# Rotary attention stage: exponentials of one PSUM bank each in six units, with products and pieces placed by counting banks

## The chip, the cores and the metric

One core of one Trainium2 chip. The metric is the device time of one execution in microseconds (us). Three runs of the kernel before gave 1812.57, 1814.32 and 1814.37 us, median 1814.32.

## The reference

Four layers run one after the other on x of 4 batches x 1024 tokens x 128 channels: a causal linear attention, a switch attention (expert gates on queries, keys and values), a rotary attention, and a feed-forward layer applied to the half of the tokens that a router picks. Each is added to x (the last one replaces the chosen tokens) and layer-normalised. The change lies in the third:

```python
q, k, v = (x @ W + b).reshape(B, S, 16, 8).transpose(0, 2, 1, 3)   # for Wq, Wk, Wv
q, k = apply_rope(q, rope), apply_rope(k, rope)
scores = einsum('bhqd,bhkd->bhqk', q, k) / sqrt(8)
attn = softmax(scores, axis=-1)
out = einsum('bhqk,bhkd->bhqd', attn, v)          # then @ Wo + bo
```

So 4 batches x 16 heads have a 1024 x 1024 matrix of scores each, every element of which is exponentiated.

## The kernel before

All four layers run in one program, and the rotary stage begins while the stage ahead of it ends. Its inner loop computes transposed scores: a **tile** is 128 keys by 512 queries of one head, which is one bank of PSUM (the accumulator memory: 8 banks of 128 partitions x 512 fp32). A **step** is one block of 128 keys (`kt`) against one half of the queries for a group of four heads, so four tiles. There are 8 steps for a half, 16 for a group, 64 for a batch and 256 in all: 1024 tiles.

- **TensorE scores** (`score_unit`, L2660): one matmul for a tile, of 32 rows (8 channels in four split copies) by 128 columns. The four heads of a step use the four row groups of the array, so matmuls issued together run beside each other. A *unit* is two tiles in two neighbouring banks; `unit_b` has three of them in banks 0 to 5, and the score of unit u waits for the exponential of unit u-3 (`exp_rdy`).
- **ScalarE exponentials** (L2604): one instruction of 128x1024 for a unit, out of the two banks into `probs`, a ring of four steps (16 tiles). The first unit of each step (c = 0) stands behind two waits, on `pv_done` (the ring is free) and on `score_ps` (the scores are there); the second (c = 1) has only the one on `score_ps`.
- **TensorE products** (`products`, L2674): for a step four matmuls 128 x 32 columns into the four quarters of bank 6 (`acc_b`), accumulated over the 8 key blocks of a half. They are fp32, and the trace shows each as two. The products of two steps are issued together at every even step, for the two steps before it.
- **The slot between**: at every odd step TensorE has one more item in bank 7 (`piece_b`): a `turn` (L2686, four transposes of the accumulated result, at step 3 of every 8) or a `piece`, one of the small matmul groups that prepare the next batch (its transposes, q, k, v projections), finish the batch before (project_out) or rank its tokens. The first batch also carries pieces of the stage before, two of which hold 24 matmuls (L2283). Pieces wait on `used`, which VectorE raises when it has taken the last content of bank 7.
- **VectorE** copies bank 6 to `acc` after every 8 steps (L2799), normalises, takes the pieces and does the layer norm of the batch before. **GpSimd** lays out `vg`. **SyncE** writes the rotated q and k to DRAM (L2382) and reads them back by group (L2387, `staged`), where reading waits for a count of `score_ps`.

TensorE's order in `batch`, for a step i: score unit (i, c=1), score unit (i+1, c=0); if i is even the products of steps i-2 and i-1; if i is odd the turn or piece. TensorE runs its queue in order, and so does ScalarE. Two steps (four units, eight tiles) make one **cycle** of this order, counted below from the start of one block of products to the next: products, two score units, the item of the slot, two score units.

Before the first score of the second unit, `tail.banks_left` waits until the stage before has left the banks.

Of the kernel before, what the change touches and what calls it, by code (L numbers as in the profile page):

```python
# [16 lines left out]
ACT = mybir.ActivationFunctionType  # L17
# [2284 lines left out]
class RotaryLead:  # L2302
# [5 lines left out]
              + [("v", 0), ("v", 1)])  # L2308
    AT = {(0, 1): (0, 1), (0, 2): (2, 3), (0, 3): (4, 5), (1, 0): (6, 7), (1, 1): (8, 9), (1, 2): (10, 11)}
    ROPE_STEPS = 2 * 2 * 5  # L2310
    COUNTS = B * 8 * NT

    def __init__(self, nc, signals, x, ps, ident, I, tag):
        self.nc, self.x, self.I, self.ident, self.bank = nc, x, I, ident, ps[:, 0, :]
        self.base = self.end = nc.sbuf_base
        self.tag = tag
        sem, sb = signals.names(tag), self.place
        self.wq, self.wk, self.wv, self.wo, self.wq_sw, self.wk_sw = (sb(n, [P, D]) for n in ("wq", "wk", "wv", "wo", "wq_sw", "wk_sw"))
        self.b_col = sb("b_col", [P, 4])
        self.b_all = sb("b_all", [P, 2, D])  # L2320
        self.spared = self.end - self.base
        self.cos, self.sin = sb("cos", [P, T]), sb("sin", [P, T])
        self.xT = sb("xT", [P, T])
        self.rot, self.part = sb("rot", [P, HALF]), sb("part", [P, HALF])
        self.split = sb("split", [P, 4, T], F32R)
        self.keys = sb("keys", [P, 2, T], F32R)
        self.queries = sb("queries", [P, 2, T], F32R)
        self.vg = [sb("vg0", [P, NT, self.G, 32])]
        self.v = sb("v", [P, B * NT, D])
        self.needs = self.end - 4 * (B - 1) * NT * D  # L2330
        self.vg.append(sb("vg1", [P, NT, self.G, 32]))
        self.probs = sb("probs", [P, 4, 2, 2, HALF])
        self.acc, self.ao = sb("acc", [P, 2, HALF]), sb("ao", [P, NT, D])
        self.needs_later = self.end
        self.heads = nc.dram_tensor(tag + "heads", [B, 2, H, 4, HD, T], F32).ap()
# [113 lines left out]
def rotary_led(nc, x, ps, ident, place, signals, lead, tail, weights_of, recips, flag, I, tag):  # L2449
# [25 lines left out]
    with ctx:  # L2475
# [26 lines left out]
        SC = 2 * STEPS  # L2502
        NORM_STEPS = LN_STEPS + 1
        ROPE_STEPS = lead.ROPE_STEPS
        DMAS = 2
# [14 lines left out]
        def pieces(b, first, last):  # L2520
# [9 lines left out]
                at.update({PIECE_STEPS[NZ + NX + k]: (d_index(b, k), kind, half, b - 1) for k, (kind, half) in enumerate(D_PIECES)})  # L2530
            return at

        def turned_at(b, i):

            return b * NP + (i - TURN) // NT if i >= TURN else max(b * NP - 1, 0)
# [71 lines left out]
        def _(pe):  # L2607
            pe.sem_inc(score_ps, ONE + SC)
            pe.sem_inc(pv_done, ONE + STEPS)
            def piece(index, kind, half, b, turned=0):  # L2610

# [34 lines left out]
            def score_unit(step, c):  # L2646

                b, i = step // BS, step % BS
                g, half, kt = i // STEPS, i // NT % 2, i % NT
                par, u = g % 2, 2 * step + c  # L2650
                if i % STEPS == 0 and c == 0:
                    pe.wait_ge(staged[par], 16 * DMAS * (b * (NG // 2) + g // 2 + 1))

                if u == 1:
# [3 lines left out]
                for s in range(2):  # L2658
                    at = 32 * (2 * c + s)
                    last = nc.tensor.matmul(unit_b[u % NU][:, s, :], keys[at:at + 32, par, kt * P:(kt + 1) * P], queries[at:at + 32, par, half * HALF:(half + 1) * HALF], start=True, stop=True)  # L2660
                last.then_inc(score_ps, 1)

            def products(b, i):

                par, kt, pair = i // STEPS % 2, i % NT, i // NT
                pe.wait_ge(exp_rdy, ONE + 2 * (b * BS + i) + 2)
                if i % STEPS == 0:
                    pe.wait_ge(vg_rdy, ONE + G * (b * NG + i // STEPS + 1))
                if kt == 0:

                    pe.wait_ge(acc_sb, ONE + b * NP + pair)
                for hh in range(G):
                    at = 32 * hh
                    last = nc.tensor.matmul(acc_b[at:at + 32, :], vg[par][:, kt, hh, :], probs[:, kt % 4, hh // 2, hh % 2, :],  # L2674
                                            start=(kt == 0), stop=(kt == NT - 1))
                last.then_inc(pv_done, 1)

# [10 lines left out]

            pe.wait_ge(used, NX)

            def batch(b, first, last):
                at = pieces(b, first, last)
                for i in range(BS):
                    step = b * BS + i
                    score_unit(step, 1)
                    if step + 1 < B * BS:
                        score_unit(step + 1, 0)
                    if i % 2 == 0 and step:
                        for back in (2, 1):
                            products(*((b, i - back) if i else (b - 1, BS - back)))  # L2700
                    if i % NT == TURN and not (first and i == TURN):
                        turn(*((b, i // NT - 1) if i > TURN else (b - 1, NP - 1)), (NX if first else z_index(b, 0)) + sum(j < i for j in at))
                    if i in at:
                        piece(*at[i], turned_at(b, i))

            score_unit(0, 0)
            batches(pe, batch)
            for back in (2, 1):
                products(B - 1, BS - back)

            def left():
                turn(B - 1, NP - 1, z_index(B, 0) - NX)
# [736 lines left out]
```

## Time and profile before

| | before |
|---|---|
| median of 3 runs | 1814.32 us |
| the profiled execution's own time | 1811.27 us |
| its span, first to last instruction | 1809.5 us |
| granted TensorE clock, mean | 0.978 |
| TensorE busy | 1661.8 us (92%) |
| ScalarE busy | 1272.4 us (70%) |
| VectorE busy | 1116.0 us (62%) |
| GpSimd busy | 893.4 us (49%) |
| first rotary exponential starts / last one starts | 1203.3 / 1719.9 us |

The profile is of one execution. Times are in us from the start of the span unless they are marked ns. PE is TensorE's matmuls, PEld its weight loads, ACT ScalarE, DVE VectorE, POOL GpSimd, SP SyncE. Busy shares are means over stages with different limits; the rotary stage lies between 1203 and 1723. A matmul counts as busy until its last column is written, so TensorE reads as busy while it only finishes. Two neighbouring ScalarE instructions overlap in the records, because the end of one is still being written when the next one starts; the distance from start to start is what an instruction costs there.

### The profile page before, as it was taken

How to read it: one execution, taken by the hardware profiler on the slowest of the kernel's cores; microseconds unless marked ns; L12 is line 12 of the kernel's file. 1: busy time of each engine (PE TensorE's matmuls, PEld its weight loads, DVE VectorE, ACT ScalarE, POOL GpSimd, SP SyncE). 2: the span in 40 equal slices, each digit the busy share in tenths (PEclk: the TensorE clock that was granted, in tenths of full speed). 3: DMA queues.
4: the chain of work that ended last, by engine and by line, in shares of the span. 5: the costliest groups of instructions: out<-in, count | busy, mean ns of one | idle time of the engine just before them, and what ended most of it. 6: DMA issues, size and time to landing. Idle time of an engine off the chain costs nothing. (4 is left out here: it accounts for less than half of the span.)

```text
span 1809.5 us, 29276 instructions
## 1 busy us (share of the span) xinstructions
PE 1661.8 (92%) x10754; PEld 883.5 (49%) x10754; DVE 1116.0 (62%) x1920; ACT 1272.4 (70%) x2447; POOL 893.4 (49%) x621
## 2 busy tenths in 40 slices
PE   7989479999999999999999999779999999998995
PEld 4556355555565555655555555324333333332364
DVE  4669669787678796787976667531413344251365
ACT  4554126867676758676767576678999999999943
POOL 3456456887766788757787577850000000000052
PEclk8999789999999999999999999989999999999998
DMA  3000222221111112111112110130220401311001
GB/s 84 2 12 2 105 68 78 70 75 59 43 59 43 56 46 64 38 57 45 56 46 68 34 59 21 54 133 24 70 95 24 140 24 58 106 34 51 1 12 38
DMA packets 38791, 97.56 MB, mean 54 GB/s; under 512 B 5040, under 2 KB 16496, under 8 KB 38512
## 3 DMA queue, kind: packets, MB, share of 16 engines
q1 hardware_dynamic: 38640, 95.59, 16.9%
q8 instruction: 90, 1.47, 0.3%
q14 instruction: 61, 0.50, 0.1%
HBM read 49.96 MB, written 28.84 MB: 44 GB/s over the span
## 5 line engine op out<-in xcount | busy, mean ns | idle before, releaser
L1133 POOL TENSOR_TENSOR b_psum<-b_psum,b_probs 128x1024 f32<-128x1024 f32 x192 | 460.7, 2400 | 213.5 <-ACT b_probs L1293 207.2
L2604 ACT ACTIVATE c_probs<-banks 128x1024 f32<-128x1024 f32 x512 | 483.6, 1029 | 37.1 <-PE banks L2660 21.5
L1293 ACT ACTIVATE b_probs<-banks 128x1024 f32<-128x1024 f32 x256 | 255.8, 1023 | 215.7 <-PE banks L1439 215.4
L1649 DVE TENSOR_TENSOR b_gated<-banks,b_g 128x480 f32<-128x480 f32 x512 | 310.8, 653 | 137.7 <-PE banks L1404 129.1
L1404 PE MATMUL banks<-b_w,b_xh 128*128 128x480 f32 x1024 | 353.4, 398 | 37.4 <-ACT b_probs L1293 15.7
L1665 DVE TENSOR_REDUCE b_tok<-b_gated 128x192 f32<-128x960 f32 x248 | 272.3, 1138 | 0.3
L1262 ACT ACTIVATE b_share<-b_o,b_picked 128x64 f32<-128x64 f32 x1080 | 269.3, 343 | 1.7 <-DVE b_o L1690 1.7
L1404 PEld LDWEIGHTS banks<-b_w,b_xh 128*128 128x128 f32 x1024 | 194.8, 190 | 119.0 <-issue 59.8
L2674 PE MATMUL banks<-c_probs,c_vg 128*32 128x512 f32 x2048 | 248.7, 603 | 3.0 <-DVEq L2725 2.6
L1474 PE MATMUL banks<-b_probs,b_tok 128*64 128x512 f32 x1024 | 248.3, 605 | 2.6 <-ACT b_probs L1293 2.6
L1439 PE MATMUL banks<-b_qq,b_kk 64*128 64x512 f32 x1536 | 228.2, 421 | 5.9 <-DVE b_gated L1649 5.5
L2589 POOL COPY c_vg<-c_v 128x64 f32<-128x64 f32 x60 | 12.8, 258 | 415.5 <-PE banks L2674 366.8
L2660 PE MATMUL banks<-c_queries,c_keys 32*128 32x512 f32 x1024 | 176.2, 500 | 25.1 <-ACT c_probs L2604 18.3
L1404 PE MATMUL banks<-b_w,b_xl 128*128 128x480 f32 x512 | 196.1, 383 | 0.0
L1439 PEld LDWEIGHTS banks<-b_qq,b_kk 64*128 64x128 f32 x1536 | 130.8, 185 | 76.9 <-issue 31.5
L2660 PEld LDWEIGHTS banks<-c_queries,c_keys 32*128 32x128 f32 x1024 | 68.9, 183 | 202.5 <-ACT c_probs L2604 166.0
L1144 POOL TENSOR_TENSOR b_z<-b_z,b_share 128x1280 f32<-128x1280 f32 x54 | 160.9, 2981 | 0.0
L1474 PEld LDWEIGHTS banks<-b_probs,b_tok 128*64 128x64 f32 x1024 | 62.0, 136 | 123.4 <-issue 89.6
L2674 PEld LDWEIGHTS banks<-c_probs,c_vg 128*32 128x32 f32 x2048 | 53.8, 109 | 113.0 <-issue 72.7
L1404 PEld LDWEIGHTS banks<-b_w,b_xl 128*128 128x128 f32 x512 | 97.8, 191 | 9.9
L1133 POOL TENSOR_TENSOR b_psum<-b_probs 128x1024 f32<-128x1024 f32 x32 | 76.9, 2402 | 34.3 <-ACT b_probs L1293 34.3
L821 DVE TENSOR_TENSOR a_weights<-banks,a_later 128x512 f32<-128x512 f32 x96 | 60.2, 682 | 41.3 <-PE banks L731 41.1
(282 smaller groups left out, 1793.7 us busy)
## 6 DMA issues: line engine op xcount, KB each, us to landing
b_w<-b_split_w SPq DMA_DIRECT2D x24, 960.0 KB, 4.7
b_kk<-b_kk SPq DMA_DIRECT2D x64, 256.0 KB, 3.7
c_heads<-c_split SPq DMA_DIRECT2D x24, 512.0 KB
c_keys<-c_heads SPq DMA_DIRECT2D x16, 512.0 KB, 4.1
c_queries<-c_heads SPq DMA_DIRECT2D x16, 512.0 KB, 5.3
b_split_w<-b_w SPq DMA_DIRECT2D x8, 960.0 KB, 6.0
b_raw_w<-in_L_ffn_W SPq DMA_DIRECT2D x8, 480.0 KB, 4.0
c_heads<-c_split SPq DMA_DIRECT2D x8, 384.0 KB
```

Of the source, the lines that this page charges most:

```text
L1133: nc.gpsimd.tensor_tensor(psum[:, par, :], prev, probs[:, i % 4, :], ALU.add).then_inc(psum_rdy, 1)
L1144: nc.gpsimd.tensor_tensor(zf, zf, sf, ALU.add).then_inc(z_rdy[half], 1)
L1262: nc.scalar.activation(dst[:, e, :], o[:, t, :], ACT.Copy, scale=picked[:, b % 2, t, h * E + e:h * E + e + 1]).then_inc(share_rdy, 1)
L1293: nc.scalar.activation(probs[:, i % 4, :], score_b[i % 2], ACT.Exp).then_inc(exp_rdy, 1)
L1404: last = nc.tensor.matmul(proj_b[u % WAYS][:, 0:HALF_W], a[:, x_of % 2, t * P:(t + 1) * P], w[:, par, part, j, :], start=(i == 0), stop=(i ...
L1439: last = nc.tensor.matmul(score_b[i % 2][:, lo:hi], kk[rows, par, k_part, (side + i) % 2, i // 2 * P:(i // 2 + 1) * P], qq[rows, par, q_pa ...
L1474: last = nc.tensor.matmul(acc_b[DH * half:DH * half + DH, :], tok[:, n % 4, 2, i, :], probs[:, i % 4, lo:hi], start=(i == 0), stop=(i == N ...
L1649: nc.vector.tensor_tensor(shape(gated[:, t % 2, j, :]), shape(proj_b[u % WAYS][:, 0:HALF_W]), g.unsqueeze(2).broadcast_to([P, 3, HD2, E]), ...
L1665: nc.vector.tensor_reduce(tok[:, n % 4, :, t, :].rearrange("p j (f d) -> p f j d", f=2), gated[:, t % 2, :, :].rearrange("p f (j d e) -> p ...
L2604: nc.scalar.activation(probs[:, step % 4, c, :, :], unit_b[u % NU], ACT.Exp, scale=float(HD) ** -0.5).then_inc(exp_rdy, 1)
L2660: last = nc.tensor.matmul(unit_b[u % NU][:, s, :], keys[at:at + 32, par, kt * P:(kt + 1) * P], queries[at:at + 32, par, half * HALF:(half ...
L2674: last = nc.tensor.matmul(acc_b[at:at + 32, :], vg[par][:, kt, hh, :], probs[:, kt % 4, hh // 2, hh % 2, :], start=(kt == 0), stop=(kt == ...
```

## The change

The unit becomes `WIDE` = 1 tile in one bank, and there are `NU` = 6 of them in the same banks 0 to 5. The exponential takes 128x512, so 1024 of them stand where 512 stood. `probs` is now a ring of `RING` = 16 tiles, of the same size as before. The waits of ScalarE, TensorE and SyncE count tiles. Each exponential from tile 16 on has both waits ahead of it. The score of tile u waits for the exponential of tile u-6. TensorE's order is written as one loop over units: products of the two steps of pair p follow the score of tile 8p+13 (`first_unit`), and the item of the slot follows the score of tile 8p+17, four scores later. `tail.banks_left` is now waited for ahead of the first score.

```diff
-    NU = 3
+    NU, WIDE, RING = 6, lead.WIDE, lead.RING
+    TILES = B * BS * G
+    UNITS = -(-TILES // WIDE)
-        self.probs = sb("probs", [P, 4, 2, 2, HALF])
+        self.probs = sb("probs", [P, self.RING, HALF])
-        unit_b = [ps[:, 2 * k:2 * k + 2, :] for k in range(NU)]
+        unit_b = [ps[:, WIDE * k:WIDE * (k + 1), :] for k in range(NU)]
...
             def stage(b, g):
-                sp.wait_ge(score_ps, ONE + SC * (b * NG + g))
+                if b * NG + g > 1:
+                    sp.wait_ge(score_ps, ONE + units_for((b * NG + g - 1) * STEPS * G))
...
         def _(act):
-            for step in range(B * BS):
-                act.wait_ge(pv_done, ONE + STEPS - 3 + step)
-                for c in range(2):
-                    u = 2 * step + c
-                    act.wait_ge(score_ps, ONE + SC + u + 1)
-                    nc.scalar.activation(probs[:, step % 4, c, :, :], unit_b[u % NU], ACT.Exp, scale=float(HD) ** -0.5).then_inc(exp_rdy, 1)
+            for u in range(UNITS):
+                n, slot = len(tiles_of(u)), WIDE * u % RING
+                spent = tiles_of(u)[-1] - RING
+                if spent >= 0:
+                    act.wait_ge(pv_done, ONE + STEPS + spent // G + 1)
+                act.wait_ge(score_ps, ONE + u + 1)
+                nc.scalar.activation(probs[:, slot:slot + n, :], unit_b[u % NU][:, 0:n, :], ACT.Exp, scale=float(HD) ** -0.5).then_inc(exp_rdy, 1)
...
+            def score_unit(u):
+                if u == 0:
                     tail.banks_left(pe)
                 if u >= NU:
                     pe.wait_ge(exp_rdy, ONE + u - NU + 1)
+                for n in tiles_of(u):
...
+                    last = nc.tensor.matmul(unit_b[u % NU][:, n % WIDE, :], keys[...], queries[...], start=True, stop=True)
                 last.then_inc(score_ps, 1)
             def products(b, i):
-                pe.wait_ge(exp_rdy, ONE + 2 * (b * BS + i) + 2)
+                pe.wait_ge(exp_rdy, ONE + units_for(G * (b * BS + i + 1)))
...
-                for i in range(BS):
-                    step = b * BS + i
-                    score_unit(step, 1)
-                    if step + 1 < B * BS:
-                        score_unit(step + 1, 0)
-                    if i % 2 == 0 and step:
-                        for back in (2, 1):
-                            products(*((b, i - back) if i else (b - 1, BS - back)))
...
+            def first_unit(pair):
+                return -(-(2 * G * (pair + 1)) // WIDE) + NU - 1
+            pair = 0
+            for u in range(UNITS):
+                score_unit(u)
+                if u == first_unit(pair):
+                    for step in (2 * pair, 2 * pair + 1):
+                        products(step // BS, step % BS)
+                    pair += 1
+                if pair and u == first_unit(pair - 1) + G:
+                    between(2 * pair + 1)
```

## Rows read from the trace of the kernel before

**Rows 1.** The page's costliest groups; busy us, mean ns | idle before it.

```profile
L2604 ACT ACTIVATE c_probs<-banks 128x1024 f32<-128x1024 f32 x512 | 483.6, 1029 | 37.1 <-PE banks L2660 21.5
...
L2674 PE MATMUL banks<-c_probs,c_vg 128*32 128x512 f32 x2048 | 248.7, 603 | 3.0 <-DVEq L2725 2.6
```

**Rows 2.** Busy time by stretch: whole loop; five cycles with pieces; eight nearly without.

```profile
core 0: us, PE busy (x) PEld busy (x) DVE busy (x) ACT busy (x) POOL busy (x), PEclk, DMA share, GB/s
1210.52:1717.53 507.01, 477.42 (x3449) 169.94 (x3449) 169.96 (x399) 473.77 (x502) 21.34 (x60) 0.99 0.18 58
1391.94:1411.45 19.51, 19.41 (x134) 6.28 (x132) 8.55 (x15) 18.86 (x21) 0.76 (x4) 1.00 0.23 75
1635.56:1666.80 31.24, 27.09 (x203) 8.66 (x201) 2.48 (x6) 30.18 (x33) 0.77 (x4) 1.00 0.16 53
```

**Rows 3.** Timeline of one cycle, TensorE: start us, us, engine, line, count.

```profile
1399.75 1.92 PE L2674 MATMUL banks<-c_probs,c_vg 128*32 128x512 f32 x16
...
1401.60 0.50 PE L2660 MATMUL banks<-c_queries,c_keys 32*128 32x512 f32 x4
...
1402.04 1.12 PE L2623 MATMUL banks<-c_xT,c_wq_sw 128*128 128x512 f32 x2
...
1403.09 0.63 PE L2660 MATMUL banks<-c_queries,c_keys 32*128 32x512 f32 x4
...
1403.65 1.92 PE L2674 MATMUL banks<-c_probs,c_vg 128*32 128x512 f32 x16
```

**Rows 4.** The same cycle on ScalarE, one exponential at a time.

```profile
1399.16 1.02 ACT L2604 ACTIVATE c_probs<-banks 128x1024 f32<-128x1024 f32 x1
...
1400.07 1.03 ACT L2604 ACTIVATE c_probs<-banks 128x1024 f32<-128x1024 f32 x1
...
1400.97 1.04 ACT L2604 ACTIVATE c_probs<-banks 128x1024 f32<-128x1024 f32 x1
...
1402.14 1.02 ACT L2604 ACTIVATE c_probs<-banks 128x1024 f32<-128x1024 f32 x1
...
1403.06 1.02 ACT L2604 ACTIVATE c_probs<-banks 128x1024 f32<-128x1024 f32 x1
```

**Rows 5.** Timeline, TensorE: the last score pair of that cycle alone.

```profile
1403.22 0.50 PE L2660 MATMUL banks<-c_queries,c_keys 32*128 32x512 f32 x2
```

**Rows 6.** Timeline around a stall at a group's first step.

```profile
1309.08 0.50 PE L2660 MATMUL banks<-c_queries,c_keys 32*128 32x512 f32 x2 [1.35 <-DMA c_queries<-c_heads]
...
1309.68 1.02 ACT L2604 ACTIVATE c_probs<-banks 128x1024 f32<-128x1024 f32 x1 [0.88 <-PE banks L2660]
```

**Rows 7.** ScalarE groups by form: busy us, mean ns | idle before it.

```profile
L616 ACT COPY a_weights<-banks 128x512 f32<-128x512 f32 x32 | 18.6, 582 | 18.4 <-PE banks L731 18.4
...
L593 ACT COPY a_share_rows<-banks 128x128 f32<-128x128 f32 x4 | 1.1, 266 | 1.4 <-PE banks L696 1.3
...
L578 ACT ACTIVATE a_relu<-banks,a_bk 128x512 f32<-128x512 f32 x8 | 5.6, 695 | 2.9 <-PE banks L670 2.9
```

**Rows 8.** Timeline, ScalarE: two instructions in a row after an idle stretch.

```profile
1722.69 1.07 ACT L2996 COPY d_xT<-banks 128x512 f32<-128x512 f32 x2 [0.44 <-PE banks L3058]
...
1380.37 1.94 ACT L2604 ACTIVATE c_probs<-banks 128x1024 f32<-128x1024 f32 x2 [1.01 <-PE banks L2660]
```

**Rows 9.** Timeline: long piece of the first batch; a piece behind VectorE.

```profile
1234.09 4.30 PE L2283 MATMUL banks<-b_wo,b_zT 128*128 128x128 f32 x24
...
1379.26 0.63 PE L2635 MATMUL banks<-ident,r 128*128 128x128 f32 x4 [1.87 <-DVE c_xT L2737]
```

**Rows 10.** Timeline: the first products, and the next exponentials.

```profile
1210.52 3.64 PE L2674 MATMUL banks<-c_probs,c_vg 128*32 128x512 f32 x16 [2.61 <-DVEq L2725]
...
1214.68 3.77 ACT L2604 ACTIVATE c_probs<-banks 128x1024 f32<-128x1024 f32 x4 [4.86 <-PE banks L2660]
```

**Rows 11.** Timeline: the last products, and VectorE's copy of their result.

```profile
1719.81 2.26 PE L2674 MATMUL banks<-c_probs,c_vg 128*32 128x512 f32 x16
...
1722.42 0.69 DVE L2799 COPY c_acc<-banks 128x512 f32<-128x512 f32 x1
```

More of the change, by code:

```diff
@@ L2310 @@
     ROPE_STEPS = 2 * 2 * 5
+    WIDE, RING = 1, 16
     COUNTS = B * 8 * NT
@@ L2498, in rotary_led @@
         score_ps, exp_rdy, pv_done, acc_sb, accT_ps, recip_rdy, ao_rdy, norm_steps = map(sem, ("score_ps", "exp", "pv", "acc_sb", "accT_ps", "recip_rdy", "ao_rdy", "norm_steps"))
-        unit_b = [ps[:, 2 * k:2 * k + 2, :] for k in range(NU)]
+        unit_b = [ps[:, WIDE * k:WIDE * (k + 1), :] for k in range(NU)]
         acc_b, piece_b = ps[:, 6, :], ps[:, 7, :]
-        SC = 2 * STEPS
         NORM_STEPS = LN_STEPS + 1
@@ L2531, in pieces, with tiles_of, units_for @@
             return at
+        def tiles_of(u):
+            return range(WIDE * u, min(WIDE * (u + 1), TILES))
+        def units_for(tiles):
+            return -(-tiles // WIDE)
         def turned_at(b, i):
@@ L2597, in _ @@
             act.sem_inc(exp_rdy, ONE)
-            for step in range(B * BS):
-                act.wait_ge(pv_done, ONE + STEPS - 3 + step)
-                for c in range(2):
-                    u = 2 * step + c
-                    act.wait_ge(score_ps, ONE + SC + u + 1)
-                    nc.scalar.activation(probs[:, step % 4, c, :, :], unit_b[u % NU], ACT.Exp, scale=float(HD) ** -0.5).then_inc(exp_rdy, 1)
+            for u in range(UNITS):
[5 more added lines that the diff above has]
+                nc.scalar.activation(probs[:, slot:slot + n, :], unit_b[u % NU][:, 0:n, :], ACT.Exp, scale=float(HD) ** -0.5).then_inc(exp_rdy, 1)
         @block.tensor
         def _(pe):
-            pe.sem_inc(score_ps, ONE + SC)
+            pe.sem_inc(score_ps, ONE)
             pe.sem_inc(pv_done, ONE + STEPS)
@@ L2644, in piece @@
                 last.then_inc(filled, 1)
[L2646 to L2654, printed above, removed]
+            def score_unit(u):
+                if u == 0:
                     tail.banks_left(pe)
@@ L2657, in score_unit @@
                     pe.wait_ge(exp_rdy, ONE + u - NU + 1)
-                for s in range(2):
-                    at = 32 * (2 * c + s)
-                    last = nc.tensor.matmul(unit_b[u % NU][:, s, :], keys[at:at + 32, par, kt * P:(kt + 1) * P], queries[at:at + 32, par, half * HALF:(half + 1) * HALF], start=True, stop=True)
+                for n in tiles_of(u):
+                    step, hh = n // G, n % G
+                    b, i = step // BS, step % BS
+                    g, half, kt = i // STEPS, i // NT % 2, i % NT
+                    par, at = g % 2, 32 * hh
+                    if i % STEPS == 0 and hh == 0:
+                        pe.wait_ge(staged[par], 16 * DMAS * (b * (NG // 2) + g // 2 + 1))
+                    last = nc.tensor.matmul(unit_b[u % NU][:, n % WIDE, :], keys[at:at + 32, par, kt * P:(kt + 1) * P], queries[at:at + 32, par, half * HALF:(half + 1) * HALF], start=True, stop=True)
                 last.then_inc(score_ps, 1)
@@ L2673, in products @@
                     at = 32 * hh
-                    last = nc.tensor.matmul(acc_b[at:at + 32, :], vg[par][:, kt, hh, :], probs[:, kt % 4, hh // 2, hh % 2, :],
+                    last = nc.tensor.matmul(acc_b[at:at + 32, :], vg[par][:, kt, hh, :], probs[:, (G * (b * BS + i) + hh) % RING, :],
                                             start=(kt == 0), stop=(kt == NT - 1))
@@ L2689, in _, with between @@
             pe.wait_ge(used, NX)
-            def batch(b, first, last):
-                at = pieces(b, first, last)
-                for i in range(BS):
-                    step = b * BS + i
-                    score_unit(step, 1)
-                    if step + 1 < B * BS:
-                        score_unit(step + 1, 0)
-                    if i % 2 == 0 and step:
-                        for back in (2, 1):
-                            products(*((b, i - back) if i else (b - 1, BS - back)))
[L2701 to L2709, printed above, removed]
+            def between(step):
+                b, i = step // BS, step % BS
+                at = pieces(b, b == 0, b == B - 1)
+                if i % NT == TURN and step > TURN:
+                    turn(*((b, i // NT - 1) if i > TURN else (b - 1, NP - 1)), (z_index(b, 0) if b else NX) + sum(j < i for j in at))
+                if i in at:
+                    piece(*at[i], turned_at(b, i))
+            def first_unit(pair):
[9 more added lines that the diff above has]
+                    between(2 * pair + 1)
+            while 2 * pair < B * BS:
+                for step in (2 * pair, 2 * pair + 1):
+                    products(step // BS, step % BS)
+                pair += 1
             def left():
```

## The prediction

> **What bounds the kernel now.** I read the page first: ScalarE has 483.6 us of rotary exponentials with only 37.1 us of idle ahead of them, the products 3.0 us [rows 1]. That looks as if ScalarE were nearly full. The busy times by stretch say that it isn't so simple: five cycles take 19.51 us (3.90 each) with pieces in all their slots, and eight with only two turns take 31.24 us, which is 3.905 each, though TensorE then has 27.09 us of work [rows 2]. The cycle has one length whatever its slot holds, so neither engine's amount of work sets it; a loop of waits between the two does.
>
> The timelines show the loop. On ScalarE the starts lie 0.91, 0.90, 1.17 and 0.92 us apart [rows 4]: three times it runs back to back, and once in four it waits some 0.26 us, of which the page counts only the part after the overlap. In TensorE's order the cycle is products at 1399.75, four scores at 1401.60, the piece at 1402.04, scores from 1403.09, products at 1403.65 [rows 3]; the last score pair starts at 1403.22 [rows 5]. Followed round: the exponential that starts at 1402.14 ends at 1403.16, the score pair that needed its banks starts 0.06 later, products follow 0.43 after it, the next scores 1.85 after those, and the next waiting exponential 0.54 after them. 0.06 + 0.43 + 1.85 + 0.54 + 1.02 = 3.90 us, the whole cycle. The products of 1.85 us stand between a bank's release and the scores that fill it, and ScalarE has too few filled units to last over them.
>
> **The loop after the change.** Six single banks are the same reserve of scores. I follow pair p from its exponential 8p+7, which frees the bank of tile 8p+13. Its score starts 0.06 later; the products behind it 0.43 after that; tiles 8p+14 to 8p+17 1.85 later (they need exponentials 8p+8 to 8p+11, long done); exponential 8p+14 at the earliest 0.54 later. That is 2.88 us from the end of 8p+7, terms as in rows 3 to 5. Meanwhile ScalarE has exponentials 8p+8 to 8p+13. So the question is what a 512-wide exponential costs, which no row shows.
>
> Its price: copies of 512 and 128 columns take 582 and 266 ns [rows 7], so 512 columns are 0.42 us. An exponential of 1024 takes 1.02 and starts 0.90 apart back to back [rows 4]; less 0.42 that is 0.60, and 0.48 apart. Both agree with the 512-wide copy, 0.58. Two exponentials after an idle stretch take 1.94 [rows 8], less 0.84 that is 1.10; two copies of 512 take 1.07 [rows 8]; I take 1.09. ScalarE's own floor is 8 x 0.48 = 3.82 us a cycle. The upper bound, an instruction with a bias column (695 ns [rows 7], about 0.57 apart if it overlaps as much), is excluded, because the exponential has no such operand.
>
> The six exponentials in between last 6 x 0.48 = 2.87 us from the start of 8p+8, and that start lies 0.12 before the end of 8p+7. So ScalarE is dry about 0.12 us before tile 8p+14 can be ready, it starts late again, and the loop closes: exponential 8p+14 starts, 8p+15 ends 1.09 after that start, and 8p+15 is the one that the next pair's last score waits for (8(p+1)+7). The loop is 2.88 + 1.09 = 3.97 us. The exchange is plain: before, one exponential of 1.02 stood in the loop, now two short ones do, 1.09.
>
> One more term. Every exponential from tile 16 on now has two waits ahead of it, and the waiting one is such an instruction. Before, the one that waited at the products was the second of a step, with a single wait: 0.54 from the start of its scores [rows 3, 4]. The row where a first of a step waited, after the stall at 1309.08, shows 0.60 [rows 6]. So the second wait adds 0.06, here once per cycle. The forecast cycle is 2.88 + 1.09 + 0.06 = 4.03; with the third decimals that rows 3 to 8 round away I take 4.02, against 3.90: **plus 0.116 us a cycle**. The bounds: from below 2.88 + 1.07 without the second wait, less 0.02 for rounding, 3.93, plus 0.03; from above both rounded up, 4.05, plus 0.14. The nearest rows are the exponentials and the stall, so I stay near the upper one.
>
> The slot still fits: a piece of 1.05 plus 1.85 + 0.44 of products and scores ends 3.34 after the products' start, tiles 8p+18 to 8p+20 go at once, and tile 8p+21 waits until 3.53 anyway. Scores of single tiles run beside each other as pairs did (two pairs 0.13 apart took 0.63 in all [rows 3]), so they cost TensorE nothing; if they didn't overlap, half of them would add 4 x 0.43 a cycle.
>
> **How many cycles grow.** From the first products to 1717.53 there are 507.01 us [rows 2] and 126 cycles. 117 take 3.90; nine are longer, together 50.4 us. Two hold the 24-matmul piece: all exponentials are done when it ends, 4.22 after it starts [rows 9], so they stay as they are. Three wait for VectorE's layer norm before a piece, as at 1379.26 [rows 9], and one for a read of queries at 1309.08 [rows 6]. These end a fixed time after an event one or more cycles earlier, so they and the cycle before each don't grow: four plain ones less. One more is bound by VectorE's copy after three cycles (12.02 us where three of 4.02 make 12.06), so this group gains 0.04 and two plain ones more drop out. The first (5.67) gains 0.06 alone, having no second wait yet; one at a lowered clock gains 0.12. So 111 x 0.116 = 12.9, plus 0.12 + 0.06 + 0.04 = 13.1 us.
>
> The ends. `banks_left` now holds back the first score by 0.85 us. That is covered: the first products started at 1210.52, released by VectorE's queue and not by exponentials [rows 10], and 8 tiles from 1204.15 are done by 1208. Without that cover it would cost 0.85. The next exponentials at 1214.68 follow those products [rows 10], as before. At the end two short exponentials stand where one stood, plus 0.12; but VectorE's copy of the last result waits for its ranking until 1722.42, while the products ended at 1722.07 [rows 11]: 0.35 of the growth is absorbed. Sum: 13.1 + 0.12 - 0.35 = **12.9 us**.
>
> Edits with no price: SyncE's staging waits name the same scores, counted in tiles, so its reads and the writes queued behind them start in the same place of the order. `probs` keeps its 16 tiles: exponential 8p+16 starts 3.4 us after the products' start and needs only their first step, done after 1.3. The slot's items keep their steps, so GpSimd's and VectorE's waits stay; each gets 0.12 more slack a cycle. 512 more exponentials and some 750 more waits are issued by ScalarE's queue while it runs, one of each per 0.48 us.
>
> The profiled execution took 1811.27 us, 3.05 below the median of the runs shown; by the sum it would take 1824.2. Against the median 1814.32 I predict **1827.2 us**. What a measurement can tell from no change is about 0.2%, 3.6 us.
>
> **Rivals.** *Faster: ScalarE becomes the bound at its floor.* If tile 8p+14 were ready in time, 8 short exponentials of 0.48 would set the cycle, 3.82, and TensorE (1.85 + 0.44 + 1.05 + 0.44 = 3.78) just fits. 0.084 less in 112 cycles, less 0.3 at the end, is 9.1 us: 1805. It needs the 2.88 us from release to exponential to fall under 2.75, by 0.12 and by 0.06 more for the second wait. Each term repeats in every cycle of before, which speaks against it. The Trainium skill (Perfetto Trace Analysis, Optimizing Scalar/DVE Operations) says that where ScalarE isn't saturated but makes other engines wait, breaking up its instructions may let work complete sooner. By that rule the result would lie on this side; here the products wait for the second of two short ones, and the page doesn't ask for that. Chance 0.08.
>
> *The loop without surcharge.* It is the loop above, but the second wait is hidden and the short exponential is as cheap as the copy. 3.93 to 3.96 a cycle, plus 3.5 to 6.5 us: 1818 to 1821. The stall's row speaks against it; it is one row. Chance 0.12, half of it within 0.2%.
>
> *ScalarE bound at a higher price.* If the fixed part of an instruction doesn't overlap at 512 wide as at 1024, ScalarE is full. From 0.52 apart on, 8 of them pass the loop's 4.02 and 4.16 would be the cycle: 0.256 x 112 = 29 us, 1843. The starts 0.90 apart and the copies speak against it. The Trainium skill (ScalarE: Activation LUTs, What ACT_TABLE_LOAD costs) gives 186 ns + 0.833 per column with 93 ns of overlap, by which 512 columns come 0.52 apart and the time is this one. For 1024 columns it gives 0.946, where this trace has 0.90, so the trace disagrees. Chance 0.03.
>
> *The change is neutral,* because something I don't see holds the cycle at 3.90: 1814. Nothing but the nearness of 3.90 and 3.97 speaks for it. Chance 0.04. The forecast's own chance is 0.73.
>
> **The numbers.** Faster: 0.08. Within 0.2%: half of the loop without surcharge and the neutral case, 0.10. Slower: 0.82. The range runs from the low end of the loop without surcharge to 4.05 a cycle (0.14 x 112 = 15.7 us) with 1.5 for the spread of runs: 1818 to 1832. It leaves out the faster, the neutral and the higher price, 0.15.
>
> **What would show it.** In the changed profile: exponentials of 128x512 x1024 at about 0.60 us; starts 0.48 apart seven times and once about 0.67; a cycle of 4.02 with and without pieces; products 0.43 after the score of tile 8p+13; 0.60 from the scores after the products to the exponential; first products still at 1210.5. A cycle of 3.82 with no gap would make me wrong in the release-to-exponential path, 3.96 in the second wait, over 4.1 in the price of a short exponential.

## The result and the profile after

| | before | after |
|---|---|---|
| median (runs, lowest to highest) | 1813.44 us (4, 1812.2 to 1814.37) | 1825.72 us (4, 1821.53 to 1827.4) |
| ratio to before, 95% interval | | 1.0071 (1.0051 to 1.0091) |
| the profiled execution's own time | 1811.27 us | 1821.53 us |
| its span | 1809.5 us | 1819.7 us |
| first products start / last products end | 1210.52 / 1722.07 us | 1210.70 / 1733.56 us |

The change costs 12.3 us by the medians of four runs each, with 9.2 to 16.5 in the interval; 12.9 were predicted, from 1814.32 to 1827.2. The profiled pair differs by less, 10.3 us, and shows where. The stage starts 0.18 us later, the stretch from the start of the first products to the end of the last grows from 511.55 to 522.86 us (+11.31), and what follows falls from 87.4 to 86.2.

The page's costliest groups of the kernel after (busy us, mean ns | idle ahead of it) answer to [rows 1]:

```profile
L2616 ACT ACTIVATE c_probs<-banks 128x512 f32<-128x512 f32 x1024 | 514.3, 627 | 17.7 <-PE banks L2671 17.6
...
L2685 PE MATMUL banks<-c_probs,c_vg 128*32 128x512 f32 x2048 | 249.6, 605 | 1.8 <-DVEq L2743 1.6
```

ScalarE is busy 30.7 us longer, and its idle time falls from 37.1 to 17.7. A reader who stops here would call ScalarE full. The busy times by stretch of the kernel after, whole loop and then five cycles, answer to [rows 2]:

```profile
core 0: us, PE busy (x) PEld busy (x) DVE busy (x) ACT busy (x) POOL busy (x), PEclk, DMA share, GB/s
1210.70:1728.91 518.21, 510.83 (x3449) 191.00 (x3449) 170.32 (x399) 504.32 (x1006) 21.01 (x60) 0.99 0.17 57
1390.85:1410.91 20.06, 20.06 (x133) 6.67 (x132) 7.86 (x14) 20.06 (x42) 0.00 (x0) 1.00 0.04 9
```

Five cycles take 20.06 us, 4.01 each, where they took 19.51. In them both engines now read as 100% busy, and neither is at its limit: waiting and overlap are hidden in the records. Only the starts tell. TensorE's timeline of the kernel after (start, us) answers to [rows 3]; the row of x1 is the score that the products follow, seen alone:

```profile
1398.88 1.92 PE L2685 MATMUL banks<-c_probs,c_vg 128*32 128x512 f32 x16
1400.73 0.50 PE L2671 MATMUL banks<-c_queries,c_keys 32*128 32x512 f32 x4
1401.16 0.66 PE L2697 MATMUL banks<-ident,c_acc 128*128 128x128 f32 x4
1401.75 1.21 PE L2671 MATMUL banks<-c_queries,c_keys 32*128 32x512 f32 x4
...
1402.46 0.50 PE L2671 MATMUL banks<-c_queries,c_keys 32*128 32x512 f32 x1
...
1402.89 1.92 PE L2685 MATMUL banks<-c_probs,c_vg 128*32 128x512 f32 x16
```

The same cycle on ScalarE, one exponential at a time, from the first that waits to the next one that does; it answers to [rows 4]:

```profile
1401.32 0.60 ACT L2616 ACTIVATE c_probs<-banks 128x512 f32<-128x512 f32 x1
...
1401.82 0.59 ACT L2616 ACTIVATE c_probs<-banks 128x512 f32<-128x512 f32 x1
...
1402.29 0.60 ACT L2616 ACTIVATE c_probs<-banks 128x512 f32<-128x512 f32 x1
...
1402.77 0.62 ACT L2616 ACTIVATE c_probs<-banks 128x512 f32<-128x512 f32 x1
...
1404.20 0.66 ACT L2616 ACTIVATE c_probs<-banks 128x512 f32<-128x512 f32 x1
...
1404.68 0.67 ACT L2616 ACTIVATE c_probs<-banks 128x512 f32<-128x512 f32 x1
...
1405.34 0.60 ACT L2616 ACTIVATE c_probs<-banks 128x512 f32<-128x512 f32 x1
```

The loop is the predicted one. Scores behind the products at 1400.73, the waiting exponential 0.59 later at 1401.32, the next one ends at 1402.41, the score that needed its bank starts at 1402.46, the products at 1402.89: two short exponentials (1.09) where one long one (1.02) stood. Starts are 0.48 apart seven times (two that repeat the pattern are left out) and 0.66 once. But look at the durations: from the second on each is some 0.013 longer than the one before it, so the *ends* are 0.49 apart. That matters below, and it corrects the sentence ahead of the prediction that the distance from start to start is what an instruction costs.

### The profile page after: what moved, and what is told of

Same layout as the page of the kernel before. It is cut to its first block and busy times, and to the rows that moved or that the text cites. A ratio compares the mean times of both kernels' runs of the same rounds, so it can differ in the third digit from the quotient of the medians.

```text
span 1819.7 us, 30539 instructions
## 1 busy us (share of the span) xinstructions
PE 1697.2 (93%) x10754; PEld 906.1 (50%) x10754; DVE 1115.4 (61%) x1920; ACT 1302.6 (72%) x2959; POOL 891.8 (49%) x621
## 5 line engine op out<-in xcount | busy, mean ns | idle before, releaser
L2616 ACT ACTIVATE c_probs<-banks 128x512 f32<-128x512 f32 x1024 | 514.3, 627 | 17.7 <-PE banks L2671 17.6
L2671 PE MATMUL banks<-c_queries,c_keys 32*128 32x512 f32 x1024 | 210.1, 497 | 4.2 <-issue 0.8
L2671 PEld LDWEIGHTS banks<-c_queries,c_keys 32*128 32x128 f32 x1024 | 90.9, 183 | 193.8 <-ACT c_probs L2616 175.0
```

The source lines that it names most:

```text
L2616: nc.scalar.activation(probs[:, slot:slot + n, :], unit_b[u % NU][:, 0:n, :], ACT.Exp, scale=float(HD) ** -0.5).then_inc(exp_rdy, 1)
L2671: last = nc.tensor.matmul(unit_b[u % NU][:, n % WIDE, :], keys[at:at + 32, par, kt * P:(kt + 1) * P], queries[at:at + 32, par, half * HALF ...
```

## The experiments

All kernels are the one after the change with a few edits; `WIDE` 2 and `NU` 3 give back exponentials of two banks. "Loop" is the time from the start of the first products to the end of the last, "rest" what follows to the end of the span. Each is from the one profiled execution. The ratio is to runs of the kernel before on the same chip; their medians lie between 1812.77 and 1814.89. The time ahead of the first products varies by up to 7 us between the profiled executions (1210.5 to 1217.75); in e3, the latest, 4.2 of them arise already in the stage before, whose code is the same in all. So the plain cycle and the loop say more than the total. "Plain cycle" is the length that nearly all cycles have; in e5, e6, e8 and e10 it is that of the cycles in the new order (83 to 85 of 127), and the others keep 3.90 us (3.95 in e6).

| kernel | us, median | ratio (95%) | plain cycle | loop | rest |
|---|---|---|---|---|---|
| before | 1813.44 | | 3.90 | 511.55 | 87.4 |
| after | 1825.72 | 1.0071 (1.0051 to 1.0091) | 4.01 | 522.86 | 86.2 |
| e1 one bank, wait once | 1820.36 | 1.0037 (1.0022 to 1.0051) | 3.95 | 518.59 | 86.2 |
| e2 two banks, both waits | 1825.98 | 1.0064 (1.0047 to 1.0081) | 3.96 | 518.29 | 87.3 |
| e3 two banks, wait once | 1815.43 | 1.0001 (0.9991 to 1.001) | 3.90 | 511.02 | 86.3 |
| e4 products one score earlier | 1827.54 | 1.0067 (1.0051 to 1.0084) | 4.01 | 523.28 | 86.4 |
| e7 five units | 1903.53 | 1.0504 (1.0483 to 1.0525) | 4.50 | 603.08 | 87.8 |
| e6 one bank, mixed order | 1825.66 | 1.0078 (1.0061 to 1.0095) | 3.92 | 516.63 | 93.1 |
| e5 two banks, mixed order | 1807.49 | 0.9972 (0.9959 to 0.9985) | 3.67 | 499.26 | 93.0 |
| e8 e5, norms and ranking moved | 1800.77 | 0.9944 (0.9925 to 0.9964) | 3.67 | 502.05 | 86.1 |
| e10 e5, ranking alone moved | 1803.99 | 0.994 (0.992 to 0.9959) | 3.67 | 501.29 | 87.2 |
| e9 e3, norms and ranking moved | 1813.44 | 1.0011 (0.9999 to 1.0024) | 3.90 | 513.53 | 86.2 |

### The two terms taken apart: e1, e2, e3

The theory has two terms: two short exponentials in the loop (+0.05 a cycle) and a second wait ahead of the one that waits (+0.06). e1 takes away the wait alone: the four tiles of a step become free together, so the first tile's wait covers all.

```diff
-                if spent >= 0:
+                if spent >= 0 and tiles_of(u)[0] % G == 0:
```

e2 takes back the width alone, with both waits ahead of each exponential:

```diff
-    WIDE, RING = 1, 16
+    WIDE, RING = 2, 16
...
-    NU, WIDE, RING = 6, lead.WIDE, lead.RING
+    NU, WIDE, RING = 3, lead.WIDE, lead.RING
...
-                if pair and u == first_unit(pair - 1) + G:
+                if pair and u == first_unit(pair - 1) + G // WIDE:
```

e3 has both edits, and so keeps only the rewritten placement.

> The changed kernel, but ScalarE waits for the free ring only at the first tile of a step (every fourth exponential), so the exponential that waits behind the products has one wait, as it had before the change. Theory (a loop of waits, in which the second wait costs 0.06 us a cycle): the start from scores to the late exponential falls from 0.60 to 0.54 us, the plain cycle from 4.01 to 3.95 us, and the time by 0.06 x some 112 cycles = 6.7 us, to about 1819. Rival (ScalarE's price for twice as many instructions is all of it): cycle and time stay at 4.01 us and 1825.7. Rival (ScalarE's queue, which handles the 750 extra waits, is the limit): more than 0.1 us a cycle comes back, and the time is back at 1813.

> The changed kernel with units of two tiles (WIDE 2, three units), that is the new loop and its counting with the 1024-wide exponential of before, and both waits ahead of every exponential. Theory: the loop is 0.06 + 0.43 + 1.85 + 0.60 + 1.02 = 3.96 us, 0.06 over before, from the second wait alone: about 1820, 7 over before. Rival (the width is all of it): 3.90 and 1813.5, as before. Rival (the new placement costs by itself): 4.01 and about 1825, as the changed kernel.

> The same with units of two tiles, and the ring's wait only at the first unit of a step, as before the change. Theory: the loop of before, 3.90 us a cycle and 1813.5 us, since nothing is left of the change but its way of writing the order and the wait for the banks ahead of the first score, which is covered by the late first products. Rival (the first score's 0.85 us delay is not covered): 1814.4, the first products later. Rival (placement costs by itself): as the changed kernel, 1825.

Measured: cycles of 3.95, 3.96 and 3.90 us, each as the theory had it. From e3 to the kernel after, the second wait is 0.06 and the short exponentials 0.05, and each gives its part with the other present or absent. e3's interval holds 1, so the order "placed by banks" is free, as predicted. TensorE's timeline of e1:

```profile
1394.12 1.93 PE L2685 MATMUL banks<-c_probs,c_vg 128*32 128x512 f32 x16
...
1398.08 1.92 PE L2685 MATMUL banks<-c_probs,c_vg 128*32 128x512 f32 x16
...
1402.03 0.64 PE L2685 MATMUL banks<-c_probs,c_vg 128*32 128x512 f32 x4
```

One number of e2 was not foreseen: its time is 1825.98, not 1820. About 2.2 us of the difference are eight cycles of 4.24, exactly sixteen cycles apart. Timeline of e2 in one of them:

```profile
1371.92 0.50 PE L2671 MATMUL banks<-c_queries,c_keys 32*128 32x512 f32 x4
...
1372.81 1.94 ACT L2616 ACTIVATE c_probs<-banks 128x1024 f32<-128x1024 f32 x2 [0.47 <-PE banks L2671]
```

The exponential starts 0.89 after its scores instead of 0.60. Sixteen cycles of e2 are 128 instructions of ScalarE's queue (four exponentials and four extra waits a cycle, each of which the trace records as an instruction of its own), which may point to something at each 128th instruction. They are also two groups of heads, but e3, which has the same order on TensorE, has no such cycle. What it is was not tested. Between the medians of e3 and e2 lie 10.6 us, between their loops 7.3; the remainder stays open.

### Is it the reserve, or where the products stand? e4 and e7

e4 issues the products one score earlier, e7 has five units instead of six.

```diff
-                return -(-(2 * G * (pair + 1)) // WIDE) + NU - 1
+                return -(-(2 * G * (pair + 1)) // WIDE) + NU - 2
```

```diff
-    NU, WIDE, RING = 6, lead.WIDE, lead.RING
+    NU, WIDE, RING = 5, lead.WIDE, lead.RING
```

> The changed kernel with products and slot item one score earlier: the products of pair p follow the score of tile 8p+12 and wait for exponential 8p+7 themselves, so the 0.43 us of a score no longer stand between them, but only five filled tiles are left to last over them. Theory: after the products the late exponential is tile 8p+13, and three short ones lead to 8p+15: 0.06 + 1.85 + 0.60 + 0.49 + 0.48 + 0.60 = 4.08 us a cycle, 0.07 more than the changed kernel: about 1833. Rival (what counts is the path from the exponential to the products, 0.43 shorter): the cycle falls to ScalarE's floor of 3.82 and the time to about 1805.

> The changed kernel with five units in place of six. The run with products one score earlier came out at 4.01 us a cycle and not 4.08: the late exponential is always the one after the score that goes ahead of the products, so what stands in the loop is (tiles in a cycle) - (units) short exponentials in a row, wherever the products are put. Corrected theory: with five units three of them are in the loop, 0.06 + 0.43 + 1.85 + 0.60 + 0.49 + 0.48 + 0.60 = 4.51 us a cycle, 0.50 more than the changed kernel in some 113 cycles: about 1881. Rival (ScalarE's price of a short exponential bounds the cycle): five units still cover most of the products, the cycle stays near 4.01 and the time near 1825.

e4 missed its expectation on both sides: 4.01, no change. What I had overlooked: if the products follow the score of tile 8p+12, the late exponential is that of 8p+13, and the next products follow the score of 8p+20, which waits for exponential 8p+14. In the change the same three are 8p+14, 8p+21 and 8p+15. Eight tiles a cycle less six units is two exponentials in the loop, wherever the block is cut. e7 confirms this with three: 4.01 + 0.49 = 4.50. TensorE's timeline of e7:

```profile
1417.94 1.92 PE L2685 MATMUL banks<-c_probs,c_vg 128*32 128x512 f32 x16
...
1422.44 1.92 PE L2685 MATMUL banks<-c_probs,c_vg 128*32 128x512 f32 x16
...
1425.32 1.70 PE L2671 MATMUL banks<-c_queries,c_keys 32*128 32x512 f32 x4
1426.95 0.64 PE L2685 MATMUL banks<-c_probs,c_vg 128*32 128x512 f32 x4
```

Its time is 22 us above the expected one. Some fifteen of its cycles take 5.7 to 6.8 us, and the granted clock of its loop is 0.95, where it was 0.99; between 1719 and 1757 us it is 0.82. Timeline of e7 there:

```profile
1749.07 1.50 PE L2671 MATMUL banks<-c_queries,c_keys 32*128 32x512 f32 x3 [0.51 <-ACT c_probs L2616]
1750.50 3.53 PE L2685 MATMUL banks<-c_probs,c_vg 128*32 128x512 f32 x16
```

The longer loop leaves TensorE idle where the slot is empty, 0.51 us a cycle, and products behind such a wait often ran at the lower clock (3.53 us for 1.92). Often, not always: after the same wait at 1343.20 they took 1.92. That the idle time brings the clock down is argued, not shown. The page of e7 says how much idle there is ahead of ScalarE, five times that of the kernel after:

```profile
L2616 ACT ACTIVATE c_probs<-banks 128x512 f32<-128x512 f32 x1024 | 515.4, 625 | 96.7 <-PE banks L2671 96.7
```

### Breaking the loop: e5 and e6

If 1.85 us of products in one block are what ScalarE can't bridge, the two steps of products should be placed apart. In these two kernels, in cycles whose slot is empty or holds a short item (a turn), TensorE does: products of one step, the item, four scores, products of the other step, four scores. Cycles with a long piece stay as they were.

```diff
...
+                here.append((products, 2 * pair))
+                if item < B * BS and short(item):
+                    here.append((between, item))
+                    later.append((products, 2 * pair + 1))
+                else:
+                    here.append((products, 2 * pair + 1))
+                    later.append((between, item))
...
```

e5 does this on e3 (two banks), e6 on e1 (one bank).

> Units of two tiles and the ring's wait once a step (the loop of before), with another order on TensorE where the slot's item is short (four transposes) or absent, 83 of the cycles: products of one step, the item, four scores, products of the other step, four scores. There a block of products is 0.99 us and no longer 1.85, and at most 0.99 + 0.55 stands between the release of a bank and the scores that fill it: 0.06 + 0.43 + 1.54 + 0.54 = 2.57 us, under the 2.7 us of three filled units. Theory: no exponential is left in the loop, those cycles fall to ScalarE's floor of 4 x 0.905 = 3.62 us, the other 44 stay at 3.90; 83 x 0.28 = 23 us less, of which the norms and the ranking on VectorE keep some 3: about 1795. Rival (TensorE's amount of work and its changes between row and column tiling bound the cycle): 3.90 stays or grows by 0.13 a cycle, 1814 to 1825.

> The same order with the short exponentials and six units, the ring's wait once a step. Theory: the 83 cycles with a short item or none fall to the floor of short exponentials, 8 x 0.477 = 3.82 us, the other 44 stay at 3.95: against the kernel before 83 x -0.08 + some 38 x 0.05 = -5 us, about 1809, and 15 us over the same order with 1024-wide exponentials. Rival (short exponentials cost no more once the loop is open): as fast as the kernel with the wide ones, 1795.

The loop is gone in both, and what remains is ScalarE, back to back. TensorE's timeline of e5, then of e6:

```profile
1332.51 1.06 PE L2685 MATMUL banks<-c_probs,c_vg 128*32 128x512 f32 x8
...
1334.34 1.07 PE L2685 MATMUL banks<-c_probs,c_vg 128*32 128x512 f32 x8
...
1336.18 1.07 PE L2685 MATMUL banks<-c_probs,c_vg 128*32 128x512 f32 x8
```

```profile
1333.80 1.06 PE L2685 MATMUL banks<-c_probs,c_vg 128*32 128x512 f32 x8
...
1335.76 1.07 PE L2685 MATMUL banks<-c_probs,c_vg 128*32 128x512 f32 x8
...
1337.71 1.07 PE L2685 MATMUL banks<-c_probs,c_vg 128*32 128x512 f32 x8
```

Half a cycle is 1.83 and 1.955 us, so a cycle 3.67 and 3.92 (the median of the 83), where I expected 3.62 and 3.82. The line's summary in that stretch shows why, for e5 (min/median/max ns, first and last start):

```profile
L2616 ACT ACTIVATE c_probs<-banks x13: 1019/1098/1178, 1330.1 to 1340.9; 128x1024 f32<-128x1024 f32 x13
```

and for e6:

```profile
L2616 ACT ACTIVATE c_probs<-banks x19: 818/938/1058, 1333.0 to 1341.6; 128x512 f32<-128x512 f32 x19
```

In e6 the starts are 0.477 apart (8.58 / 18 with the second decimals), while the durations grow by (1058 - 818) / 18 = 13 ns each: ends 0.490 apart, and eight of them are the 3.92 of the cycle. In e5 it is 10.84 / 12 = 0.903, plus 13 ns, 0.917, and four are 3.67. While the engine runs without a pause, the cycle keeps to the ends. At 1655.24 us e6 even has one start 0.67 behind the last, while its end comes 0.489 after the end before it, like all its neighbours. So the floor of the change is 3.92, above the 3.90 that before took: **with one bank per exponential no order of its plain cycles could have been faster than before.** e6's loop is only 2 us shorter than e1's. Its total missed its expectation by 17 us, 1825.66 for 1809; it lies 18 us over e5, where 15 were expected.

e5's total missed too, 1807.49 for 1795. The loop gives 12.3 us, but the rest grew from 87 to 93. VectorE's timeline of e5 at the end:

```profile
1710.88 1.28 DVE L2825 TENSOR_SCALAR_CACHE_REDUCE c_y<-c_aoT,c_w_col 128x1024 f32<-128x1024 f32 x1
...
1713.17 1.82 DVE L2832 TENSOR_SCALAR c_weight<-c_sel 128x8 f32<-128x8 f32 x1
1715.02 0.69 DVE L2837 COPY c_acc<-banks 128x512 f32<-128x512 f32 x1
```

The last products end at 1710.45, but the copy of their result waits until 1715.02 behind the last batch's ranking. And the stalls at the two layer norms grow, since TensorE now reaches the piece sooner: their cycles take 8.55 and 8.34 us for 5.23 and 5.21 before. Behind each the products run at the lower clock (1.94 us for 1.06 in these rows):

```profile
1368.20 1.06 PE L2685 MATMUL banks<-c_probs,c_vg 128*32 128x512 f32 x8
1372.66 0.63 PE L2647 MATMUL banks<-ident,r 128*128 128x128 f32 x4 [3.39 <-DVE c_xT L2775]
1373.21 0.77 PE L2671 MATMUL banks<-c_queries,c_keys 32*128 32x512 f32 x4
1373.91 1.94 PE L2685 MATMUL banks<-c_probs,c_vg 128*32 128x512 f32 x8
```

### What follows the loop: e8, e9, e10

e8 moves the layer norms four steps later and the last batch's finishing pieces and ranking earlier; e9 does the same to e3, as a control; e10 has only the last batch's part.

```diff
-    NORM_AT = 14
+    NORM_AT = 18
...
-    RANK_AT, RANK_STEPS = 57, NT + 4
-    TAIL_NORM = 30
+    RANK_AT, RANK_STEPS = (57, 57, 57, 37), NT + 4
+    TAIL_NORM = 34
...
-                at.update({PIECE_STEPS[NZ + NX + k]: (d_index(b, k), kind, half, b - 1) for k, (kind, half) in enumerate(D_PIECES)})
+                at.update({PIECE_STEPS[(8 if last else NZ + NX) + k]: (d_index(b, k), kind, half, b - 1) for k, (kind, half) in enumerate(D_PIECES)})
...
```

> The mixed order with 1024-wide exponentials, and three pieces of VectorE's work moved: the layer norm of a batch from step 14 to step 18 and that of the stage before from step 30 to 34, so that no piece of TensorE waits behind them, and in the last batch the router's pieces and the ranking from steps 47 to 61 to steps 25 to 41. Theory: the mixed order took 13 us out of the loop of products, and lost some 10 us of it again where a piece waits for the norm (two waits of about 4.9 us over a cycle's length) and had the last result wait 4.6 us behind the ranking. Without these the time is about 15 us lower than the mixed order, 1792. Rival (the norm then delays another piece or the copy of bank 6 by as much): 1800 to 1807.

> The same three moves alone, on the kernel with units of two tiles and the order of before (3.90 us a cycle). Theory: VectorE's work binds only three or four cycles there (1.1 to 1.3 us each) and 0.35 us at the end, so the moves bring about 4 us: 1810 where the kernel before has 1813 to 1815. Rival (the moves and not the order are what makes the mixed kernel fast): as fast as the mixed order with the moves.

> The mixed order with exponentials of two banks and the waits once a step, as in e5 (span 1803.5), and of the moves of e8 only those that bear on the end: the last batch's pieces and its ranking on VectorE come earlier, and the layer norms stand where e5 has them. Theory (the end of e5 waited for VectorE's ranking of the last batch, and the stalls at the layer norms only change place when the norms are moved): the part after the last products is back at about 89 us from 96, the loop stays near 496 us: span about 1797, time about 1799, as e8 (1800.8) or 1 to 2 below it. Rival (the pieces moved forward take back what the end gains, as moved norms did): span stays at 1803, with a longer loop.

The end is repaired in both (rest 86.1 and 87.2), and e8 at 1800.77 and e10 at 1803.99 beat the kernel before by 0.6%, each on its own chip. All three missed what was expected of them. e8 missed its 1792: the stalls only moved to the next piece. TensorE's timeline of e8:

```profile
1281.45 1.92 PE L2685 MATMUL banks<-c_probs,c_vg 128*32 128x512 f32 x16
1283.31 0.51 PE L2671 MATMUL banks<-c_queries,c_keys 32*128 32x512 f32 x4
1287.72 2.08 PE L2635 MATMUL banks<-c_xT,c_wq 128*128 128x512 f32 x2 [3.91 <-DVE c_ao L2849]
1289.73 0.80 PE L2671 MATMUL banks<-c_queries,c_keys 32*128 32x512 f32 x4
1290.45 2.97 PE L2685 MATMUL banks<-c_probs,c_vg 128*32 128x512 f32 x16
```

A piece waits 3.91 us for VectorE, and the matmuls behind it run at the lower clock (products 2.97 for 1.92). e10 took 1803.99 for 1799: its loop is 2.0 us longer than e5's, where it was to stay, and 1.3 of them are a cycle at the lower clock (5.22 at 1309.76) that e5 doesn't have. It is within 0.8 us of e8's loop, so moving the norms by four steps made no difference; that it is each norm's being one block on VectorE that costs is argued, since norms cut into parts were not tried. e9 took 1813.44 for 1810 and gained nothing: without the mixed order the end had only 0.35 to give, and its loop grew by 2.5.

## Why the prediction was right

**The cycle.** Predicted 2.88 + 1.09 + 0.06, taken as 4.02, plus 0.116. Between products 116 cycles are plain in both kernels: they went from 3.903 to 4.012, **plus 0.109**. The terms read 0.595 from scores to exponential (predicted 0.60), 1.085 for the two short ones (1.09), 0.05 from their end to the score (0.06), and 0.43 and 1.85 as before. e1 and e2 show the two surcharges one by one. The 0.007 that the forecast had too much lies mostly in one term: with a single wait the exponential starts 0.532 after its scores in e1 and 0.541 in e3, so the scores of single tiles let it start 0.01 earlier.

**The count.** 111 x 0.116 was predicted, and 0.22 for the special cycles, 13.1 in all; measured from first to last products' start +11.2. The plain ones give 116 x 0.109 = 12.6, the other ten gave back 1.5. That 12.9 came so near the medians' 12.3 is in part luck: in the profiled pair the loop's start to start gives 1.9 less than the sum, and the whole span grew by 10.3. The step of the count that failed is "these end a fixed time after an event one or more cycles earlier, so they don't grow". It held for the two long pieces (6.95 and 6.95, before 6.96 and 6.95). The stall at 1309.08 [rows 6] shrank instead. The read's issue on SyncE's queue in the kernel before, then the issue and the score in the kernel after:

```profile
1302.02 1.54 SPq L2387 DMA_DIRECT2D c_queries<-c_heads  x1
```

```profile
1303.07 2.11 SPq L2388 DMA_DIRECT2D c_queries<-c_heads  x1
...
1310.08 0.50 PE L2671 MATMUL banks<-c_queries,c_keys 32*128 32x512 f32 x2 [0.45 <-DMA c_queries<-c_heads]
```

The read took 7.0 us from issue to the score that it released, as before (issued at 1302.02, score at 1309.08). But TensorE came 1.9 us later while the issue came only 1.05 later, so 0.45 of stall are left of 1.35, and the clock didn't fall behind it: the two cycles went from 6.61 + 4.48 to 4.72 + 4.00. In return it fell once behind a layer norm, where it had not:

```profile
1381.19 3.32 PE L2685 MATMUL banks<-c_probs,c_vg 128*32 128x512 f32 x16
```

That cycle took 5.65 for 3.90; the granted clock is 0.56 between 1381.19 and 1384.44, mostly the lower of its two levels (1.2 GHz). The same cycle does so in e3 (5.51) and e4 (5.66), and in e1 it is one behind another layer norm (5.62), so it isn't tied to the width. Neither of the two changes of clock was forecast, and they offset each other in part: -2.4 us at the stall, +1.75 here. Four further cycles that wait for VectorE shrank by 0.14 to 0.24 each: their event lies far enough back to gain a little from every cycle.

**The ends.** `banks_left` ahead of the first score: first products at 1210.70, again released by VectorE's queue (the row reads `<-DVEq L2743`), predicted 1210.5. The next exponential at 1214.81, before 1214.68. At the end the last products grew by 4.65 - 4.54 = 0.11 (0.12 predicted), and VectorE's copy now waits for them and no longer for its ranking:

```profile
1733.70 0.69 DVE L2817 COPY c_acc<-banks 128x512 f32<-128x512 f32 x1 [0.27 <-PE banks L2685]
```

The copy starts 11.28 us later than before [rows 11] while the products end 11.49 later: 0.21 absorbed, predicted 0.35. What follows it is 1.1 us shorter than in before. e1, e3 and e9 have a rest of 86.2 to 86.3 like the kernel after, so it may be before's one profiled execution that is long (e2 and e10 have 87.3 and 87.2); why stays open.

**Edits with no price.** e3 holds the new placement, staging waits and ring, and its cycle and time are those of before. That the scores of single tiles cost TensorE nothing shows in the four of them at 1400.73, 0.50 us for all.

**The rivals.** The loop without surcharge is e1's cycle, 3.95: it needed the second wait to be hidden, and it isn't. ScalarE bound at 0.52 apart fell with the ends at 0.49. The neutral case fell with the interval, which begins at 1.0051. The Trainium skill (Perfetto Trace Analysis, Optimizing Scalar/DVE Operations) says that breaking up instructions may let work complete sooner where ScalarE isn't saturated and makes others wait. It did not here: by e1 the broken-up exponentials alone cost 0.05 a cycle. The faster rival had a term wrong in the prediction itself: "ScalarE's own floor is 8 x 0.48 = 3.82". It is 3.92 by e6, because 0.48 is the distance of the starts. So its 1805 could not have come about. The forecast didn't rest on this term, since ScalarE has 4.01 - 3.92 = 0.09 us to spare in each cycle; the expectations of e5 and e6 did, and missed by it.

## What to carry to other kernels

Where two engines hold each other up through a ring of buffers, write down the loop: the instruction that is late, the longest block that the other engine puts between release and refill, and how many instructions of the first stand between (work units per cycle less units of reserve). Finer units leave the reserve in bytes as it was and put more fixed parts and more waits into the loop; splitting the *long block* (here the products of two steps) breaks it, for 12 us in the loop of e5. And after a gain in a loop, read what stood just behind it: the wait for the ranking at the end took back 5.6 of the 12, and the two layer norms had already kept 6.5 us in the loop (8.55 + 8.34 for 5.23 + 5.21).

## What the runs showed of the hardware

- ScalarE without a pause: exponentials of 128x512 come 0.489 us apart (four per half cycle of e6, 3.91 / 8) and of 128x1024 0.917 (two per half cycle of e5, 3.67 / 4), by their ends; their starts are 0.477 and 0.903 apart, and the recorded duration grows by 13 ns with each, in most stretches until the engine next waits. So 512 more columns cost 0.428 us (0.84 ns each), and an instruction's fixed part is, by this estimate, about 0.06. The Trainium skill (ScalarE: Activation LUTs, What ACT_TABLE_LOAD costs) gives 0.833 ns a column, with which these runs agree, and a fixed part less overlap of 93 ns, which they put 30 ns lower.
- A second wait ahead of an instruction that waits anyway costs 0.06 us (e1 and e2 against the kernels with and without it). Ahead of one that runs back to back it costs nothing that shows.
- In e2 the waiting exponential was 0.3 us later once in sixteen cycles, which are 128 instructions of ScalarE's queue; the plain cycles of the other kernels don't show it, and the cause is open.
- All eight waits of TensorE for VectorE of 3.1 to 3.9 us (e5, e6, e8, e9, e10) and the two of 2.0 in e8 were followed by products at the lower clock (2.97 us for 1.92 in e8, granted clock 0.57). Of the twelve of 1.6 to 1.9 us in the kernels before and after and in e1 to e4 only four were (3.32 in the kernel after), and neither of the two in the kernel before. In e7 some waits of 0.51 were and others not. So the length of the one wait doesn't decide it, and what does stays open.
